# Between scan and experts of a gated Mamba + mixture-of-experts block on one core: who does the last splits, the routing steps and the sums, and in which order

## The reference, cut to what matters

```python
x = x + tanh(g_xattn) * ssm(ctx, z=layernorm(x))      # scan over 256 steps, 256 channels, 16 states
h = layernorm(x)                                      # [1024, 256]
logits = h @ gate_w                                   # [1024, 8]
top_logits, top_idx = top_k(logits, 2)
cw[t, top_idx] = softmax(top_logits)
for e in range(8):
    out += cw[:, e:e+1] * ((silu(h @ w0[e]) * (h @ w1[e])) @ wo[e])    # w0, w1: [256, 512], wo: [512, 256]
x = x + tanh(g_ffn) * out
```

## Time and profile before

| | us |
|---|---|
| median of 3 runs | 315.19 (313.74 to 315.58) |
| the profiled execution | 316.63 |
| its span, first to last instruction | 314.9 |
| TensorE busy / VectorE / ScalarE / GpSimd | 266.2 / 230.8 / 179.8 / 177.5 |
| mean granted clock of TensorE | 0.919 of 2.4 GHz |

### The profile page before, as it was taken

The page is one execution under the profiler, slowest core; times in us unless marked ns, Lnnn a source line. Parts: engine busy times, 40 slices in busy tenths (PEclk is TensorE's granted clock), DMA queues, the critical chain, the costliest instruction groups (busy, mean ns, idle before and its releaser), DMA issues.

```text
span 314.9 us, 4621 instructions
## 1 busy us (share of the span) xinstructions
PE 266.2 (85%) x1139; PEld 176.7 (56%) x1140; DVE 230.8 (73%) x423; ACT 179.8 (57%) x335; POOL 177.5 (56%) x159
## 2 busy tenths in 40 slices
PE   3957569869977998898799398999999999999970
PEld 3522133224332533463547276889889898898860
DVE  2775997999889999999887993565655656556540
ACT  1396477767566677557482852474564655646540
POOL 5000337997899899999675033246455464554331
PEclk9988558999999999999879857999999999999985
DMA  6599400000000000001069511042332432423312
GB/s 199 184 370 387 153 1 0 0 3 0 0 0 1 0 3 0 0 0 68 2 200 323 210 37 34 17 69 39 63 59 41 67 47 53 67 35 65 35 18 33
DMA packets 18911, 22.70 MB, mean 72 GB/s; under 512 B 2624, under 2 KB 14062, under 8 KB 18894
## 3 DMA queue, kind: packets, MB, share of 16 engines
q1 hardware_dynamic: 13312, 16.39, 15.1%
q0 software_dynamic: 4416, 6.03, 12.0%
q10 hardware_dynamic: 1166, 0.08, 0.2%
HBM read 17.38 MB, written 5.11 MB: 71 GB/s over the span
## 4 chain that ended last, share of the span: by engine, by line
PE 58%; DVE 19%; issue 9%; POOL 4%; ACT 4%; DMA 3%; POOLq 1%; SPq 0%; DVEq 0%; ACTq 0%
PE PZ L976 11%; PE PD L940 11%; PE PU L940 10%; PE PY L779 10%; DVE states L1116 5%; DVE states L1122 4%; POOL hC L403 3%; PE PY L962 3%; DMA xs<-in_x 3%; PE PU L768 2%; DVE W_lo L1213 2%; PE PY L738 2%; PE PZ L933 1%; PE PU L917 1%; PE PZ L827 1%
## 5 line engine op out<-in xcount | busy, mean ns | idle before, releaser
L403 POOL TENSOR_TENSOR hC<-states,WO 128x512 f32<-128x512 f32 x64 | 80.8, 1274 | 21.8 <-PE PY L779 14.7
L1122 DVE TENSOR_TENSOR_SCAN states<-PD,states 128x512 f32<-128x512 f32 x64 | 77.4, 1210 | 1.0 <-ACT PD L577 1.0
L779 PE MATMUL PY<-hC,ident 128*128 128x512 f32 x128 | 71.2, 644 | 6.0 <-POOL hC L403 5.9
L438 POOL DMA_INDIRECT out<-lg,y_at x23 | 36.4, 1584 | 54.5 <-ACT lg L670 49.0
L577 ACT ACTIVATE PD<-WO,Aneg 128x510 f32<-128x510 f32 x64 | 43.9, 689 | 22.2 <-DVE states L1122 18.0
L1359 DVE TENSOR_TENSOR WO_lo<-WO,WO_hi 128x512 fp32r<-128x512 f32 x46 | 29.8, 688 | 34.5 <-ACT WO_hi L663 33.9
L663 ACT ACTIVATE WO_hi<-WO 128x512 fp32r x46 | 26.5, 624 | 48.5 <-PE PZ L976 46.8
L1116 DVE TENSOR_TENSOR states<-PU,WO 128x512 f32<-128x512 f32 x64 | 42.8, 670 | 4.8 <-POOL hC L403 3.1
L425 POOL DMA_INDIRECT hC<-x_rows,x_at x23 | 23.2, 1008 | 27.2 <-DVE x_at L1329 14.9
L779 PEld LDWEIGHTS PY<-hC,ident 128*128 128x128 f32 x128 | 23.0, 200 | 22.4 <-POOL hC L403 15.6
L394 POOL TENSOR_TENSOR W_lo<-W,W_hi 128x512 fp32r<-128x512 f32 x23 | 29.2, 1275 | 0.0
(11 more groups left out here) (226 smaller groups left out, 509.7 us busy)
## 6 DMA issues: line engine op xcount, KB each, us to landing
...
hC<-x_rows,x_at POOLq DMA_INDIRECT x23, 2.8
out<-lg,y_at POOLq DMA_INDIRECT x23, 3.8
```

What stands on the lines that cost most here:

```text
L403: pool.tensor_tensor(hC[:, n % 2, :], states[:, n % RING, :], C_rep[:, pair % C_RING, :], ALU.mult).then_inc(hc_done, 1)
L438: pool.indirect_dma_start(out=out, out_offset=bass.IndirectOffsetOnAxis(ap=y_at[:, s:s + 1], axis=0), in_=y_tile[s % 2], in_offset=None, c ...
L779: pe.matmul(PY[:, h, :], ident[:, :], hC[:, n % 2, :], start=False, stop=(m == DS - 1)).then_inc(y_done, 1)
L1122: dve.tensor_tensor_scan(states[:, n % RING, :], DEC[n % 2], states[:, n % RING, :], 0.0, ALU.mult, ALU.add).then_inc(scan_done, 1)
```

## The change: what it does

- The block sums of the ranks are made by a scan on VectorE over the mask (upto) and added up in PSUM by TensorE, with `before` now 0 and -1; places has no copy, subtraction and addition for them, and adds 128 times the first slot at once, so that slot and row fall out of one number. The cast of the chosen indices goes.
- The statistics of the last two blocks stand in the gaps of places, one by one. The reciprocal group of the second half (normed(1)) stands behind all of row_hot, which now has four pieces; that of the first half stands behind the gating.
- Of the 32 splits, 18 are in the scan; five more upper parts are made by ScalarE within it. GpSimd has 4 behind the scan and 3 after row_f; VectorE 1 and 2; TensorE does four as a difference in PSUM (low_part), copied by ScalarE behind all upper parts. The fourth reuses the first's bank.
- The product of step 63 with C is VectorE's (last_hc). add_x(1, 0) stands after step 59, add_x(1, 1) behind step 63. Only one warming matmul is left.
- The products for x_at stand ahead of the two slot_w products. SP loads the first WO blocks only when hC of step 62 is done.
- WO_hi and WO_lo have two buffers each (the second lies over xs, so ScalarE waits for `stored`); gate waits for xT_lo only at its fifth matmul; in the last step down(21) stands between gate(22) and up(22), and the result of slot 21 is scaled earlier.

```diff
-ADD_X_AT, ADD_GZ_AT, X2_OUT_AT = ((48, 49), (61, 62)), (50, 51), (55, 56)
+ADD_X_AT, ADD_GZ_AT, X2_OUT_AT = (48, 49), (50, 51), (55, 56)
+ADD_NEXT_AT = 59
 ROUTER_AT, LOGITS_AT, STATS_AT = 57, 60, (56, 57, 59)
 UNROLL = 6
 
-WARM = (1, 3, 1)
+WARM = 1
 SPLITS = tuple((w, e, k) for w, experts in ((1, range(6)), (0, range(E)), (1, range(6, E))) for e in experts for k in range(2))
-SPLIT_AT = tuple(range(4, 60, 3))
-POOL_SPLITS = len(SPLIT_AT) + 4
-DVE_SPLITS = (POOL_SPLITS, POOL_SPLITS + 2, len(SPLITS))
+SPLIT_AT = tuple(range(4, 58, 3))
+EARLY = len(SPLIT_AT)
+UPPER_AT = (56, 57, 59, 60, 62)
+POOL_SPLITS = tuple(range(EARLY, EARLY + 4)) + tuple(range(EARLY + 9, EARLY + 12))
+PE_SPLITS = tuple(range(EARLY + 5, EARLY + 9))
+DVE_SPLITS = (EARLY + 4,) + tuple(range(EARLY + 12, len(SPLITS)))
...
-        WO_hi, WO_lo = (overlay(n, [P, 4, DX], at_u + b * 4 * DX * 4) for n, b in (("WO_hi", 0), ("WO_lo", 1)))
+        WO_hi, WO_lo = ([overlay(f"{n}{i}", [P, 4, DX], at + b * 4 * DX * 4) for i, at in enumerate((at_u, at_xs))]
+                        for n, b in (("WO_hi", 0), ("WO_lo", 1)))
...
-        TABLE, WARMED = bank[3], bank[4]
+        TABLE = bank[3]
+        SPLIT = [bank[i] for i in (4, 0, 1, 4)]
...
+            sp.wait_ge(hc_done, NT - 1)
             sp.wait_ge(exp_done, NT)
             sp.wait_ge(dbu_done, NT)
             load_WO(0)
             load_WO(1)
-            sp.wait_ge(hc_done, NT)
+            sp.wait_ge(last_hc, 1)
...
-            times_C(DU_AT[1], NT)
-
-            for i in range(len(SPLIT_AT), POOL_SPLITS):
+            times_C(DU_AT[1], NT - 1)
+
+            for i in POOL_SPLITS[:4]:
                 lower(i)
-
+            pool.wait_ge(row_f_ok, 1)
+            for i in POOL_SPLITS[4:]:
+                lower(i)
...
+                    if n in UPPER_AT:
+                        upper(EARLY + UPPER_AT.index(n))
...
-            for i in range(len(SPLIT_AT), len(SPLIT_AT) + 2):
-                upper(i)
             normed(range(QBLK))
-            for i in range(len(SPLIT_AT) + 2, DVE_SPLITS[1]):
-                upper(i)
             x2_out(2)
             x2_out(3)
+            for i in range(EARLY + len(UPPER_AT), EARLY + 9):
+                upper(i)
             root(1)
             normed(range(QBLK, NBLK))
             act.wait_ge(gap_ok, 1)
             act.activation(egap[:, :], gap[:, :], ACT.Exp).then_inc(egap_ok, 1)
-            for i in range(DVE_SPLITS[1], DVE_SPLITS[2]):
+            for i in range(EARLY + 9, len(SPLITS)):
                 upper(i)
+            for j in range(len(PE_SPLITS)):
+                act.wait_ge(W_lo_ps, j + 1)
+                act.activation(lo_part(PE_SPLITS[j]), SPLIT[j], ACT.Copy).then_inc(W_lo_act, 1)
...
+            act.wait_ge(stored, 16 * NQ)
...
+                if not (isinstance(s, int) and s < 2):
+                    act.wait_ge(y_ps, s - 1)
...
+            for s in range(SLOTS - 3, SLOTS - 1):
                 expert_tile(s, s % 2, 16 * ((s - 1) // 2))
+            y_out_of_bank(SLOTS - 2, SLOTS % 2, 16 * ((SLOTS - 2) // 2))
+            hidT_out(SLOTS - 1, (SLOTS - 1) % 2)
...
+                if n == NT - 1:
+                    pe.wait_ge(last_hc, 1)
+                else:
+                    pe.wait_ge(hc_done, n + 1)
...
+                pe.matmul(RANKS[:, 0:E * NBLK], before[:, :], mask[:, :, :].rearrange("p e t -> p (e t)"), start=True, stop=False)
+                pe.wait_ge(mask_sum, 1)
+                pe.matmul(RANKS[:, 0:E * NBLK], ones[:, :], upto[:, :, :].rearrange("p e t -> p (e t)"), start=False, stop=False)
+                pe.matmul(RANKS[:, E * NBLK:E * NBLK + E], ones[:, :], upto[:, :, NBLK - 1], start=False, stop=True).then_inc(rank_ps, 1)
...
+            through(at, ADD_NEXT_AT + 1)
+            add_x(1, 0)
+            through(ADD_NEXT_AT + 1, NT)
+            add_x(1, 1)
...
+            def low_part(j):
+
+                i = PE_SPLITS[j]
+                pe.wait_ge(W_hi_ok, i + 1)
+                if j >= 3:
+                    pe.wait_ge(W_lo_act, j - 2)
+                pe.matmul(SPLIT[j], ident[:, :], whole_part(i), start=True, stop=False)
+                pe.matmul(SPLIT[j], neg_id[:, :], hi_part(i).bitcast(F32), start=False, stop=True).then_inc(W_lo_ps, 1)
...
-            keep_warm(WARM[0])
             ranks()
-            keep_warm(WARM[1])
+            pe.wait_ge(neg_ok, 2)
+            pe.wait_ge(gz_ok, 2 * NQ)
+            pe.wait_ge(logits_ok, 2 * NQ)
+            for j in range(3):
+                low_part(j)
+            for _ in range(WARM):
+                pe.matmul(bank[5], ident[:, :], W1_hi[:, 0, 0, :].bitcast(F32), start=True, stop=True)
...
-            keep_warm(WARM[2])
+            low_part(3)
...
-                pe.wait_ge(xT_split, s + 1)
+                pe.wait_ge(xT_ok, s + 1)
...
+                    if split is not None and n == 4:
+                        pe.wait_ge(xT_split, split)
...
+            last = expert_of(SLOTS - 1)
+            hid_turn(SLOTS - 2, 1)
+            gate(SLOTS - 1, 0, last)
+            down(SLOTS - 2, 1)
+            up(SLOTS - 1, 0, last)
...
             def places():
 
+                n = NQ * TOPK * QBLK
                 dve.wait_ge(rank_ps, 1)
                 dve.wait_ge(consts, 15)
+                count = RANKS[:, E * NBLK:E * NBLK + E].rearrange("p (e o) -> p e o", o=1).to_broadcast((P, E, NBLK))
+                exceeded = mark(dve.tensor_tensor(over[:, :, :], count, iota_k[:, :, :], ALU.is_gt))
+                row_stat(6)
                 need(exceeded)
                 tiled = mark(dve.tensor_reduce(tiles[:, :], over[:, :, :], AX_X, ALU.add))
+                row_stat(7)
                 need(tiled)
                 ends = mark(dve.tensor_tensor_scan(tile_end[:, :], ones[:, 0:E], tiles[:, :], 0.0, ALU.mult, ALU.add))
+                dve.wait_ge(stats2_ok, 2 * QBLK + 1 + QBLK)
+                dve.bn_aggr(mv[:, 1, 4, :], stats[:, 1, 4, :]).then_inc(stats2_ok, 1)
                 need(ends)
                 starts = mark(dve.tensor_tensor(first_slot[:, :], tile_end[:, :], tiles[:, :], ALU.subtract))
+                dve.bn_aggr(mv[:, 1, 5, :], stats[:, 1, 5, :]).then_inc(stats2_ok, 1)
+                need(starts)
+                placed = mark(dve.scalar_tensor_tensor(out=rank[:, :, :].rearrange("p t e -> p e t"), in0=first_slot[:, :].rearrange("p (e o) -> p e o", o=1).to_broadcast((P, E, NBLK)),
+                                                       scalar=float(P), in1=RANKS[:, 0:E * NBLK].rearrange("p (e t) -> p e t", e=E), op0=ALU.mult, op1=ALU.add))
+                dve.bn_aggr(mv[:, 1, 6, :], stats[:, 1, 6, :]).then_inc(stats2_ok, 1)
+                need(placed)
+                at_all = rank[:, :, :].rearrange("p (q t) e -> p q (t e)", q=NQ)
+                for k in range(TOPK):
+                    chosen = mark(dve.tensor_tensor(picked[:, :, k, :, :].rearrange("p q t e -> p q (t e)"), hot[:, :, k, :, :].rearrange("p q t e -> p q (t e)"), at_all, ALU.mult))
+                dve.bn_aggr(mv[:, 1, 7, :], stats[:, 1, 7, :]).then_inc(stats2_ok, 1)
+                need(chosen)
+                summed = mark(dve.tensor_reduce(rank_f[:, :, :, :].rearrange("p q k t -> p (q k t)"), picked[:, :, :, :, :].rearrange("p q k t e -> p (q k t) e"), AX_X, ALU.add))
+                dve.wait_ge(stats2_ok, 2 * QBLK + 1 + 2 * QBLK)
+                dve.tensor_scalar(vare[:, 1, QBLK:], mv[:, 1, QBLK:, 1], EPS, None, ALU.add).then_inc(stats2_ok, 1)
+                need(summed)
+                whole = mark(dve.tensor_copy(rank_i[:, :, :, :], rank_f[:, :, :, :]))
+                need(whole)
+                in_tile = mark(dve.tensor_scalar(row_i[:, :, :, :], rank_i[:, :, :, :], P - 1, None, ALU.bitwise_and))
+                slots = mark(dve.tensor_scalar(tile_i[:, :, :, :], rank_i[:, :, :, :], P.bit_length() - 1, None, ALU.logical_shift_right))
+                need(in_tile)
+                dve.tensor_copy(row_f[:, :, :, :], row_i[:, :, :, :]).then_inc(row_f_ok, 1)
+                need(slots)
+                link(dve.tensor_copy(slot_of[:, :], tile_i[:, :, :, :].rearrange("p q k t -> p (q k t)")))
+                wide = lambda t: t.rearrange("p (n o) -> p n o", o=1).to_broadcast((P, n, COLS))
+                dve.tensor_tensor(slot_w[:, 0, :, :], iota_c[:, :, :].to_broadcast((P, n, COLS)), wide(slot_of[:, :]), ALU.is_equal).then_inc(slot_hot_ok, 1)
+                rows_hot(0)
+                dve.wait_ge(slot_hot_ok, 1)
+                dve.tensor_tensor(slot_id[:, :, :], slot_w[:, 0, :, :].bitcast(F32), wide(result_id[:, :, :, :].rearrange("p q k t -> p (q k t)")), ALU.mult).then_inc(slot_id_ok, 1)
+                for j in range(1, 4):
+                    rows_hot(j)
+                normed(1)
                 dve.wait_ge(rstd2_ok, 2 * NQ)
                 dve.tensor_tensor(gap[:, :], gap[:, :], rstd[:, 1, :], ALU.mult).then_inc(gap_ok, 1)
...
-            normed(0)
+            dve.wait_ge(c_ok, NT // 2)
```

(13 more changed lines are left out.)

188 lines of the change are left out of this document (65 added, 123 removed).

## The result

The changed kernel took **317.41 us** (median of 20 executions, 314.52 to 319.28), the kernel before 314.44 us (20, 312.43 to 317.35). The ratio is **1.0085, 95% interval 1.0056 to 1.0115**: slower by 2.7 us, and the interval allows 1.8 to 3.6. Forecast were +3.8 us and 319.0. The profiled execution took 319.07 us (span 317.2), the one before 316.63 (span 314.9).

A forecast was written before the change was run, and what follows sets the result against it. TensorE was taken to bound the expert loop, and VectorE the routing ahead of it. A first gate 4.1 us later less 0.3 in the tail gave +3.8, thus 319.0 us, with an 8-in-10 range of 315.0 to 320.6.

The forecast's parts named there:

- End of the scan: Scan end to router: moved residual sums and VectorE's step 63 product make the second half's logits about 0.8 us later.
- VectorE's routing chain: Logits to row_hot on VectorE: 2.4 us shorter, so row_hot ends at 178.3, 1.6 earlier, with nobody waiting for it.
- The wait in its place: After row_hot: late reciprocals delay ScalarE's normalisations and exponent; VectorE stands still from 178.7 to 182.2.
- The drain on top of a table load: ScalarE's table loads: a possible drain of about 1.38 us each, left out; with it the time would be 2.8 us higher.
- Behind it on VectorE: VectorE after the exponent: six small steps of 1.3 us in all, then the x_at steps; spare starts at about 183.5.
- It costs nothing as long as the weights are late: GpSimd's first gather, starting near 187.4: its data land before TensorE comes to the turn of x at 192.3.
- ScalarE to TensorE and back: Upper parts, split copy at 185.4, fourth split at half clock to 188.9, its copy, Silu load, WO's upper half to 192.3.
- the rival of the split that wakes the clock: Fourth split raises the clock and it stays; gate at 192.8, +1.5 us in all, 316.7; chance 15%.
- The gate: First gate product starts at 193.6, 4.1 us later than at 189.47.
- Loop and tail: Expert loop and end: step stays 4.88 us; the reordered last step gives -0.3 us (0 to -0.6).

The follow-up runs named there:

- e1: The changed kernel with the second half's reciprocal group and gap product moved back ahead of slot_w; 314.16 us, ratio 0.9967 to the kernel before.
- e4: The kernel before with only the loop and tail edits: double WO buffers, later wait for xT_lo, new last-step order; at most 0.47% slower by the interval.
- e5: The kernel before with the second half's reciprocal group and gap product moved behind row_hot; slower than the kernel before by 1.3%.
- e2: The changed kernel with the fourth split in its own bank, ahead of the table; gate 0.35 us later than in the changed kernel.
- e6: The changed kernel with six matmuls of no use between the table and the fourth split; ratio 1.0064 to the kernel before.
- e11: e8 plus matmuls of no use behind the table and around the turn of x, and an earlier wait for ScalarE's last split copy; 310.79 us, ratio 0.9842.
- e8: The changed kernel with early reciprocal group, fourth split in its own bank, GpSimd's late splits on VectorE, no warming matmul, earlier WO loads and first split copy; 311.38 us.

## Why the prediction was right, and where it was not

- *End of the scan.* Right in size, and lucky in the clock. From the end of the last scan step on VectorE to the second half's logits it was 7.69 us, 0.89 more than the 6.80 before (forecast 0.8), with the clock low from 155 to about 161 in both traces. In e1, which has the same code there and the clock at 1.00 all along, it was 5.24 us, against 5.08 for the old order in e4, also at 1.00: then the new order costs 0.16. The logits' place, 168.89 (forecast 168.8), was 163.29 in e1.
- *VectorE's routing chain.* Right: slot_w at 174.99 and the end of row_hot at 178.34 (178.3), 1.6 us earlier than before, though the logits came 0.9 later. Worth nothing, as forecast.
- *The wait in its place.* Right, and it carries the loss: exponent and splits at 182.13 and 182.25 (182.15), a wait of 3.46 us (3.5), with e5 and e1 as the proof in both directions. Both table loads took 1.28 us, and the next ACTIVATE began 0.01 and 0.02 us behind them. The drain on top of a table load that the Trainium skill (ScalarE: Activation LUTs, What ACT_TABLE_LOAD costs) counts did not show in the changed kernel either.
- *Behind it on VectorE: mis-sized.* The prediction gave six small steps 1.3 us, and spare a start at 183.5. It was 186.68: three of the steps took 1.2 us each instead of 0.17. It counted GpSimd's three splits as work in front of the gather and not as work beside VectorE. So the gather started at 188.24 instead of 187.4. "It costs nothing as long as the weights are late" did not help, since the weights were early: the turn waited 0.36 us for the gather's data, and e2 and e6 ran into this chain. It changed little in the sum, because the other chain ended as late.
- *ScalarE to TensorE and back.* Right as a chain: the copy at 184.84, the split at 185.56 (185.4) at half clock, the copy of it at 189.21 (189.1), the table load at 189.82 (189.8). Wrong in one term: the weights took 2.42 us instead of 3.4, since the clock rose at 188.9. This is the rival of the split that wakes the clock, half true: the clock did rise and the gate came at 192.87, where that rival had it (192.8), held by WO's upper half; but the clock did not last to the gate, whose six records took 2.92 us, as long as before, and 1.66 in e11. Nor does it always rise there: in e1 it fell during the same split and stayed at 0.50 from 178 to 188, with TensorE busy for 9.0 of those 10 us. The Trainium skill (TensorE: Matmul & The Clock Gate, What's actually happening) says that activity releases the throttled state: the changed kernel's trace agrees at 188.9, and e1's does not.
- *The gate.* 193.6 forecast, 192.87 measured: +3.4 instead of +4.1, of which 0.6 is the later start of the table's origin.
- *Loop and tail.* The step stayed (30.00 of 30 us busy). The tail was mis-sized: about -1.0 instead of -0.3. ScalarE's copy of y comes 0.47 us earlier in each step of the changed loop (the first 6.33 us behind the turn of hid, against 6.80), and the last one 0.61. So the profiled sum is +3.4 - 1.0 = +2.4, against +2.3 by the two spans (317.2 and 314.9), and +2.7 by the ratio. Two misses of the forecast's sum, 0.7 at the gate and 0.7 in the tail, go the same way. That the two traces come so near the ratio is partly luck, since such spans differ by several microseconds from one execution to the next.

What stays open: whether the fourth split alone is worth anything in the time, how much the loop edits gain (e4 leaves -0.25% to +0.47%), what e8's smaller edits bring, and why the clock rose behind the fourth split in one trace and not in another.
